# Ten zeroing transfers moved ahead of a loop of stores, and one small VectorE step moved ahead of another, in a graph-network layer

## The reference: what is computed

```
def ssp(v): return softplus(v) - log(2)
h   = x @ W_in2f                                    # [6250, 128]
Wij = ssp(f_ij @ W_filt1 + b_filt1) @ W_filt2 + b_filt2   # per edge
Wij = Wij * edge_weight[:, None]
agg = segment_sum(h[dst] * Wij, src, 6250)
out = ssp(agg @ W_out1 + b_out1) @ W_out2 + b_out2
y   = x + out
result = (y - mean(y)) / sqrt(var(y) + 1e-5)        # per row
```

## Time and profile before

| | us |
|---|---|
| median of 3 runs | 2314.89 |
| lowest, highest | 2313.6, 2318.81 |
| the profiled execution | 2323.98 |
| its span in the trace | 2322.2 |

### The profile page before, as it was taken

One profiled execution on the slowest core, in us unless ns is written; L12 is line 12 of the kernel. 1 busy time (PEld: TensorE's weight loads), 2 busy tenths in 40 slices (PEclk: granted clock), 3 DMA queues, 4 the chain that ended last, 5 costly groups with the idle time before them and its releaser, 6 DMA issues.

```text
span 2322.2 us, 59753 instructions
## 1 busy us (share of the span) xinstructions
PE 2087.2 (90%) x15953; PEld 1711.6 (74%) x15953; DVE 1889.9 (81%) x3919; ACT 1594.5 (69%) x3812; POOL 1759.7 (76%) x1078
## 2 busy tenths in 40 slices
PE   3489999899999999898999998999989999999956
PEld 2367878787877778787878787777878787877733
DVE  6468989797988889797979788888979798988836
ACT  0377777676767767676767777777767677767616
POOL 2058888887878778787878787878878787878873
PEclk9599999999999999999999999989999999999968
DMA  6755566565656555565656555656555565656494
GB/s 225 270 94 94 96 99 101 82 101 86 92 94 99 86 89 91 91 99 88 99 83 101 93 91 91 96 86 90 94 92 97 86 101 87 96 94 93 54 223 122
DMA packets 353909, 240.67 MB, mean 104 GB/s; under 512 B 86919, under 2 KB 332786, under 8 KB 353338
## 3 DMA queue, kind: packets, MB, share of 16 engines
q0 software_dynamic: 146736, 66.85, 30.6%
q1 hardware_dynamic: 196326, 152.61, 26.2%
q10 hardware_dynamic: 10476, 16.77, 1.9%
HBM read 147.25 MB, written 88.83 MB: 102 GB/s over the span
## 4 chain that ended last, share of the span: by engine, by line
PE 43%; DMA 20%; issue 15%; POOL 12%; ACT 5%; DVE 4%; ACTq 1%; POOLq 0%; SPq 0%; DVEq 0%
DMA table<-total,index 18%; POOL table L718 12%; PE unit_psum L1826 11%; PE unit_psum L1845 9%; PE both_psum L1783 7%; PE total_psum L1796 5%; PE pre_psum L1770 5%; PE both_psum L1808 2%; PE both_psum L1779 2%; DMA h_parts<-h_out 1%; ACT h_dst L871 1%; ACT total L854 1%; DMA b_o<-in_b_o 1%; ACT out_rows L1084 1%; DVE rank L1211 0%
## 5 line engine op out<-in xcount | busy, mean ns | idle before, releaser
L718 POOL DMA_INDIRECT table<-total,index x1019 | 1701.0, 1669 | 505.5 <-issue 347.2
L1826 PE MATMUL unit_psum<-moving,route_hot 128*128 128x258 f32 x3808 | 629.6, 305 | 85.5 <-ACT ring L895 79.3
L1826 PEld LDWEIGHTS unit_psum<-moving,route_hot 128*128 128x128 f32 x3808 | 517.2, 199 | 160.9 <-ACT ring L895 117.2
L895 ACT ACTIVATE ring<-unit_psum 128x258 fp32r<-128x258 f32 x952 | 355.2, 394 | 253.0 <-PE unit_psum L1826 229.9
L871 ACT ACTIVATE h_dst<-both_psum,cols 128x128 f32<-128x128 f32 x1564 | 444.6, 372 | 102.0 <-PE both_psum L1808 100.0
L1379 DVE TENSOR_SCALAR scat_hot<-node_iota,ring 128x448 fp32r<-128x448 uint16 x952 | 430.1, 471 | 61.1 <-ACT ring L895 56.5
L1845 PE MATMUL unit_psum<-scat_hot,ring 64*128 64x448 f32 x3808 | 462.7, 380 | 9.6 <-DVE scat_hot L1379 5.0
L1783 PEld LDWEIGHTS both_psum<-w_f,hidden 128*128 128x128 f32 x3128 | 429.8, 199 | 12.2
L1783 PE MATMUL both_psum<-w_f,hidden 128*128 128x128 f32 x3128 | 426.4, 281 | 0.0
L1362 DVE TENSOR_SCALAR route_hot<-node_iota,cols 128x896 fp32r<-128x896 uint16 x544 | 379.9, 716 | 42.3 <-PE unit_psum L1826 41.9
L1845 PEld LDWEIGHTS unit_psum<-scat_hot,ring 64*128 64x128 f32 x3808 | 342.6, 187 | 87.5 <-ACT ring L895 30.3
(11 more groups left out here) (118 smaller groups left out, 1500.0 us busy)
## 6 DMA issues: line engine op xcount, KB each, us to landing
dst_b<-dst SPq DMA_DIRECT2D x391, 128.0 KB
src_b<-src SPq DMA_DIRECT2D x255, 128.0 KB
f_t<-in_f_t SPq DMA_DIRECT2D x100, 256.0 KB, 3.8
table<-total,index POOLq DMA_INDIRECT x1019
table<-zeros ACTq DMA_DIRECT2D x20, 640.0 KB, 5.8
window<-h_parts SPq DMA_DIRECT2D x391, 32.0 KB
parts<-table SPq DMA_DIRECT2D x48, 256.0 KB, 5.1
h_parts<-h_out SPq DMA_DIRECT2D x12, 384.0 KB, 5.4
```

The source lines that it names most:

```text
L718: pool.indirect_dma_start(tables[table], bass.IndirectOffsetOnAxis(index[:, i, k:k + 1], 0), total[:, i, k, 0:DIM], None, compute_op=ALU.a ...
L895: act.activation(ring[:, r[1] % RING, k, :], unit_psum[:, k % 2, 0:MOVING], ACT.Copy).then_inc(ring_done, 1)
L1826: last = pe.matmul(unit_psum[:, k % 2, 0:MOVING], route_hot[:, tile, k * P:(k + 1) * P], moving[:, tile, :], start=(tile == 0), stop=(tile ...
```

## The change

Two edits, with no arithmetic changed.

```diff
             def split_h(c, tiles):            # on ScalarE
                 b = c[1] % 2
                 if not isinstance(c[0], int):
-                    for k in range(1 + b, TABLES, 2):
-                        zero(k, c[0])
+                    if b == 1:
+                        zero(2, c[0])
                 else:
                     zero(0, min(2 + c[1], FIFTHS - 1))
...
                 act.activation(h_out[:, b, 0:tiles, 1, :], h_rest[:, b, 0:tiles, :], ACT.Copy).then_inc(h_mid, 1)
+                if is_at(c, 1):
+                    act.wait_ge(edges16_stored, 32)
+                    for fifth in range(FIFTHS):
+                        zero(1, fifth)
+                        zero(3, fifth)
```

The second edit is on VectorE in the last layers:

```diff
             def last_layers(i):               # on VectorE
+                c = plus(i, -2)
+                if is_chunk(c):
+                    ...
+                    dve.wait_ge(e_inv, after_chunk(c))
+                    previous(dve, e_norm, c, after_chunk)
+                    dve.scalar_tensor_tensor(norm_shift[...], mean_var[...], -1.0, inv_dev[...], ...).then_inc(e_shift, 1)
+
                 c = i
                 if is_chunk(c):
                     ...
                     dve.wait_ge(e_pre, after_chunk(c))
                     previous(dve, e_hidden, c, after_chunk)
                     dve.tensor_scalar(soft[...], pre_psum[...], b_o1[:, 0:1], EXP_ARG_MAX, ALU.add, ALU.min).then_inc(e_clamp, 1)
-
-                c = plus(i, -2)
-                ...                           # the same shift stood here
```

More of the change, by code:

```diff
@@ L1669, in last_layers @@
             def last_layers(i):
+                c = plus(i, -2)
+                if is_chunk(c):
+                    b, tiles = c[1] % 2, tiles_of(c)
+                    dve.wait_ge(e_inv, after_chunk(c))
+                    previous(dve, e_norm, c, after_chunk)
+                    dve.scalar_tensor_tensor(norm_shift[:, b, 0:tiles], mean_var[:, b, 0:tiles, 0], -1.0,
+                                             inv_dev[:, b, 0:tiles], ALU.mult, ALU.mult).then_inc(e_shift, 1)
                 c = i
```

## The result

The changed kernel takes 2278.5 us (median of 4 runs, 2268.9 to 2280.1), the kernel before 2314.2 us beside it (median of 4). The ratio is 0.984, with a 95% interval of 0.980 to 0.987: 36 us less, where the prediction had 14.7 less.

The account below looks back on a forecast made before the run. Transfers bound the head's store loop, a ScalarE and VectorE ring the last layers' step; the edge stage stays untouched. Head -7.9 and last layers -6.8 make -14.7 us, 2314.89 to 2300.2 us; range 2293.5 to 2309.

Parts of the forecast that it names:

- The zeros in the gap: Head, behind chunk 1: ten zeroing transfers take 16.6 us of idle DMA time, end at about 60, cost nothing.
- The bound passes to the ring of a landing: Head's store loop: bound moves from bandwidth to 2.96 us of work plus a landing of 3.3; -7.9 us.
- the path that the prediction named as next and did not price: Head's store loop: TensorE's wait for the load of transposed `x`, expected to shrink with the stores' landings.
- The step without GpSimd: Last layers: with the clamp out of the ScalarE and VectorE ring, a step takes 4.29 us; three gain 0.77 each.
- The step beside GpSimd: Last layers: the shift waits for GpSimd's second addition to end, step 4.4 us; five steps gain 0.65 each.
- rival A: Last layers: shift finds no gap until GpSimd's third addition, gain there only -2.5; total -10.4, 2304.5 us; chance 0.14.
- the stricter reading: Last layers: the shift finds no gap before GpSimd's third addition, step 5.09 us, nothing won in these steps.
- Two early steps: Last layers: the step where the clamp waited for TensorE, taken as -0.9 us, and the one before, -0.3.
- The edge stage is one dependent pipeline that starts from there; I expect it to move with its start: Edge stage: it starts earlier by the head's gain and stays as long as before.
- Rival D: Edge stage: pace varies with the granted clock; settling slower would add 29 us, total +14, 2329 us; chance 0.05.

Follow-up runs that it names:

- e3: The kernel before with 8 increments of an unused semaphore on ScalarE ahead of the edge loop, no transfer moved; ratio 0.9935 to the kernel before.
- e1: The kernel before with only the zeroing edit (ten transfers together behind chunk 1), old VectorE order; ratio 0.9884 to the kernel before.
- e2: The kernel before with only the shift put ahead of the clamp in the last layers; ratio 0.9999 to the kernel before.
- e5: The kernel before with 256 semaphore increments on ScalarE ahead of the edge loop; ratio 1.0004 to the kernel before.
- e6: The kernel before with 128 semaphore increments on ScalarE ahead of the edge loop; ratio 1.0006 to the kernel before.
- e9: The kernel before with 4 semaphore increments on ScalarE ahead of the edge loop; ratio 0.9901 to the kernel before.
- e7: The changed kernel with 64 semaphore increments added on ScalarE ahead of the edge loop; ratio 0.9885 to the kernel before.
- e4: The changed kernel with 248 semaphore increments added on ScalarE ahead of the edge loop; ratio 0.9913 to the kernel before.
- e8: The changed kernel with 128 semaphore increments added on ScalarE ahead of the edge loop; ratio 0.9883 to the kernel before.
- e11: The changed kernel with the last five zeroing transfers also moved from the store loop into the burst; ratio 0.9819 to the kernel before.

## Why the prediction was wrong, point by point

**The zeros in the gap: nothing was paid, as predicted; how long they run was misread.** The sum gave all ten transfers to the gap (16.6 us, to 60), where two already ran in it before the change: eight take 13.1 us and end at about 55. ScalarE's wait for the stored lists cost nothing; its issue of ten transfers took 11.95 us and was hidden too.

**The bound passes to the ring of a landing: right for one buffer, with some luck in the number.** -8.1 against -7.9 us, and 6.2 us a pair against 6.26. But the stores landed after a median of 3.0 us, with which the sum would have given 4 x (5.27 - 3.0) = -9.1, and the other buffer waits for the load of `x`, the path that the prediction named as next and did not price.

**The step without GpSimd: right**, 4.28 against 4.29.

**The step beside GpSimd: wrong; rival A came true there.** The lock is as the prediction read it: the shift waits for the end of the running addition. The step that failed is that this is always the second addition, which gave 4.4. From the third of the six steps on it was the third addition, and those four steps have a mean of 5.06 us, where the stricter reading gave 5.09 and before had 5.06. So nothing was won beside GpSimd. The stage still gained 4.9 (6.8 predicted, 2.5 by rival A). The three steps without GpSimd gave 2.3, as predicted. Two early steps, from `hidden` at 2257.09 on, took 5.69 and 6.52 before and 4.41 and 5.16 after, 2.6 us together, where 1.2 had been put down for them. Part of that is the profiled execution of before, whose 6.52 is 5.23 and 5.24 in e3 and e1, both with the old order.

**The trace's rule against the sum.** The Trainium skill ("SBUF — State Buffer", section "SBUF: two separate sides") has a VectorE instruction with two SBUF inputs and a GpSimd instruction that reads SBUF shut each other out on a shared port. The traces agree: with two such inputs the shift ends with the addition (1.13 us), with one it takes 0.57 for the four columns beside it.

**"The edge stage is one dependent pipeline that starts from there; I expect it to move with its start": this step failed.** It was the costliest. The stage got shorter by itself: the four profiled kernels with the loop at the old place (before, e2, e5, e6) have 2115 to 2133 us, mean 2121; the ten others 2090 to 2107, mean 2099. That is 22 us, and 8.1 + 4.9 + 22 = 35 of the 36 measured (8.5 + 4.2 + 22 by the means of all stages gives the same). By the times alone the place is worth 15 us (e3) to 23 us (e9). The ScalarE wait fell from 102 to 60 us in the same means, 2.7 us for each of 16 turns, of which 1.4 reached the time. Of the rest, a part stands in waits for "issue" of the other engines, as e7 shows; the remainder was not traced.

The prediction read the chain and the windows of this stage, but not its waits. There 104.4 us before one ScalarE line, in 16 pieces of up to 8.5 us, were to be seen, as many as the loop goes back. An edit that adds instructions ahead of a loop moves the loop, and that term stood nowhere in the sum. Rival D did say that the stage's pace is not fixed, with the clock as cause and the wrong sign. The granted clock does move along: over all runs its mean is 0.944 for before and 0.948 for e3 beside it. Among the runs of one kernel, 0.001 more of it goes with some 1.3 us less, so 0.004 would be 5 us of e3's 15 (an estimate). Whether it is a cause or follows from TensorE standing still less, no run separates.

That the place decides is shown (e3, e5, e6, e9); how, is in part argued. The waits sit at the first instruction behind the taken branch. The page's queue q14 for instructions (packets, MB, share) moves packets of 1.63 MB / 200 = 8 KB:

```profile
q14 instruction: 200, 1.63, 0.2%
```

The packet records say more than this total. In all 14 traces a packet of q14 ends 0.9 to 2.9 us before ScalarE goes on, at each of the waits over 0.5 us. In the four kernels at the old place two such packets end inside the wait in 61 of 64 cases, 2.1 to 3.7 us apart, where e3 and e7 have one in nearly all. So the turn of the loop looks like a wait for fetches, and the old place like one that has to wait for two in a row. With 4 increments there are two as well, but only 0.3 to 1.9 us apart, and the wait is shorter. It is not the whole account: in e3 a second packet ends within 6 us of ScalarE's restart in 14 of 16 cases, in e4 never.

The Trainium skill ("Runtime: NRT & Kernel Launch", section "Instruction fetch mechanics") says that a taken branch whose target is not among the pages at hand waits for a fetch. The stall at each turn agrees, 2.6 to 6.6 us here. It gives refills of 16 KiB, 256 instructions. By that size the 8 KB of q14 would be 128 instructions (an estimate). The runs show a period that 128 fits, and there the measurement decides.

The other queue for instructions, q8, had 172 packets in all four kernels at the old place and in e7, and 127 to 163 in the other nine. It moves nine packets a turn or none. In after 4 of the 15 whole turns have none and take 104.2 us where the others take 106.2; in e8 it is 103.3 against 106.0. At the old place no turn is without them. Which engine this queue serves, and whether the turns are short because of it, was not tested; 4 x 2 = 8 us of the stage's gain may lie here (an estimate).

## What to carry to other kernels

Read the waits of every stage, also those that the change doesn't touch; a wait for "issue" at the first instruction of a loop, as often as the loop goes back, is a price that an edit ahead of the loop can change. When a small edit moves a large stage, repeat it with the same number of instructions that do nothing (here 8 gave -0.65%, 128 gave 0) before explaining it by what the edit does. Judge a moved instruction against what the other engine is doing at the new moment, step by step, and not by one place where it slipped through. When a stage's gain comes out near the sum, compare its parts as well: two errors may have met.

## What the runs showed of the hardware beyond that

- The turn of a loop cost ScalarE 2.6 to 6.6 us by where the loop starts in its program, with the same time for +128 and +256 instructions as for none, and another one for +4 and +8.
- Stores of 384 KB landed after 5.3 us (mean of four) when the DMA engines' share was 1.0, after 2.6 in the loop without zeros (e11), and after 3.0 in the loop with fewer zeros, where the share of the stretch from 72 to 100 us was still 0.87:

```profile
72.00:100.00 28.00, 17.05 (x62) 14.53 (x60) 12.29 (x19) 11.10 (x19) 0.00 (x0) 0.50 0.87 317
```

- Ten issues of 640 KB behind each other, onto DMA engines at a share of 1.0, took ScalarE 11.95 us, 1.2 each, where one in the loop took 0.35 (at 76.00).
- Four VectorE instructions with one-column operands took 0.57 us together, beside a working GpSimd too.
